# First attention: the causal mask moves from TensorE products to the VectorE instruction that takes the row maximum

## The reference

```
xn     = layernorm(x)
Wdkv   = xn @ latent_w + latent_b                 # keys and values, [b, 256, 36], shared by 16 heads
q      = xn @ Wd_w[h] + Wd_b[h]                   # [b, 16, 256, 36]
scores = q . Wdkv / sqrt(8), -inf where key > query
attn   = softmax(scores);  y = attn @ Wdkv;  out = concat(y) @ out_w + out_b
```

## Time and profile before

| | |
|---|---|
| median of the runs | 1755.04 us |
| span of the profiled execution, first to last instruction | 1746.9 us |
| what lies around the span (1755.04 less 1746.9) | 8.1 us |
| PE busy over the span | 1511.2 us (87%) |
| DVE busy over the span | 1119.7 us (64%) |
| ACT, POOL busy over the span | 997.0 us, 933.4 us |
| PE in the stretch 300 to 400 us (steady part of the first attention) | 98.71 us of 100 |
| DVE in the same stretch | 54.86 us of 100 |

### The profile page before, as it was taken

The page is one execution under the profiler, slowest core; times in us unless marked ns, Lnnn a source line. Parts: engine busy times, 40 slices in busy tenths (PEclk is TensorE's granted clock), DMA queues, the critical chain, the costliest instruction groups (busy, mean ns, idle before and its releaser), DMA issues. The chain is left out here.

```text
span 1746.9 us, 44836 instructions
## 1 busy us (share of the span) xinstructions
PE 1511.2 (87%) x14050; PEld 1109.0 (63%) x14051; DVE 1119.7 (64%) x2639; ACT 997.0 (57%) x2526; POOL 933.4 (53%) x1639
## 2 busy tenths in 40 slices
PE   4798999999999999998999488888888888885773
PEld 4655555555555555555998377777777777764662
DVE  3365555555555555553555399999899988985661
ACT  3343555555555555554332588888888888862441
POOL 6233555555555555554443666666666666632663
PEclk9998999999999999999999699999999999995875
DMA  7412222222222221223332021121211212116444
GB/s 197 133 29 57 55 55 55 55 55 55 56 56 56 56 56 56 56 59 75 68 70 60 22 49 45 41 44 43 46 43 41 44 44 45 42 31 123 89 90 113
DMA packets 240879, 107.53 MB, mean 62 GB/s; under 512 B 145465, under 2 KB 229242, under 8 KB 240762
## 3 DMA queue, kind: packets, MB, share of 16 engines
q1 hardware_dynamic: 230586, 93.23, 22.4%
q0 software_dynamic: 10240, 13.64, 3.7%
HBM read 61.92 MB, written 40.16 MB: 58 GB/s over the span
## 5 line engine op out<-in xcount | busy, mean ns | idle before, releaser
L670 POOL TENSOR_SCALAR_AFFINE_SELECT probs<-probs 128x512 f32<-128x512 f32 x256 | 183.5, 740 | 160.0 <-ACT probs L1515 160.0
L962 DVE TENSOR_REDUCE mneg<-bankS 128x2 f32<-128x256 f32 x256 | 107.2, 419 | 221.5 <-PE bankS L1848 220.9
L1515 ACT ACTIVATE probs<-bankT 128x1024 f32<-128x1024 f32 x128 | 131.0, 1023 | 185.2 <-PE bankT L1861 185.2
L963 DVE TENSOR_REDUCE mneg<-bankS 128x2 f32<-128x512 f32 x256 | 174.3, 681 | 0.0
L1510 ACT ACTIVATE qT<-bankA,bd 128x256 f32<-128x256 f32 x256 | 107.5, 473 | 95.0 <-PE bankA L1830 95.0
L1830 PE MATMUL bankA<-xnT,wd 128*128 128x256 f32 x512 | 149.7, 416 | 0.0
L663 POOL CAST qb<-qT 128x256 bf16<-128x256 f32 x256 | 97.1, 398 | 96.5 <-ACT qT L1510 96.3
L1858 PE MATMUL bankT<-qT,kT 37*128 37x512 f32 x512 | 136.9, 611 | 7.5 <-DMA qT<-mT 5.4
L1319 DVE STREAM_TRANSPOSE pt<-pe 128x768 f32<-128x768 f32 x128 | 124.4, 972 | 25.3 <-ACT pe L1600 25.1
L1875 PE MATMUL bankB<-probs,vaug 128*64 128x512 f32 x512 | 139.0, 621 | 1.1 <-ACT yT L1522 1.0
L1522 ACT COPY yT<-bankB 128x512 f32<-128x512 f32 x128 | 75.0, 586 | 82.1 <-PE bankB L1879 82.1
(11 more groups left out here) (316 smaller groups left out, 4315.6 us busy)
## 6 DMA issues: line engine op xcount, KB each, us to landing
rzb<-reciprocals SPq DMA_DIRECT2D x128, 128.0 KB
yT<-yT SPq DMA_DIRECT2D x64, 128.0 KB
xtab<-tab SPq DMA_DIRECT2D x32, 192.0 KB, 2.0
xs_sorted<-zeros SPq DMA_DIRECT2D x1, 4608.0 KB, 18.5
qT<-xs_sorted SPq DMA_DIRECT2D x144, 32.0 KB, 1.7
ys_sorted<-qT SPq DMA_DIRECT2D x36, 128.0 KB, 1.9
value_rows<-vrow SPq DMA_DIRECT2D x32, 128.0 KB, 1.8
vx<-value_rows SPq DMA_DIRECT2D x256, 16.0 KB, 1.8
```

Of the source, the lines that this page charges most:

```text
L670: pool.affine_select(out=blocks, in_=blocks, compare_op=ALU.is_ge, fill=0.0, base=0, pattern=[[0, 4], [1, P]], channel_multiplier=-1).then ...
L962: dve.tensor_reduce(mneg[:, n.half, :, j, 0], bankS[:, :, 0:128], AX.X, ALU.max, negate=True)
L963: dve.tensor_reduce(mneg[:, n.half, :, j, 1], bankS[:, :, 128:384], AX.X, ALU.max, negate=True).then_inc(S["red_done"], 1)
L1515: act.activation(pT[:, g % 2].rearrange("p e j t -> p e (j t)"), bankT[:, 0:2, :], ACT.Exp, scale=SCALE0).then_inc(S["exp_done"], 1)
```

## The change

The four mask products go, and with them `rowsel` and `rowneg`. A tile `future` (128 x 256, bf16; columns 0 to 127 zero, columns 128 to 255 zero or -1e30 above the diagonal) is added once, so that `future[:, 128:256]` masks the first query tile and `future[:, 0:256]` the second. `red` becomes one semaphore increment and four `tensor_tensor_reduce`, two per head, which add the mask to the scores, write the sum back to `bankS`, and write the maximum of each row, not negated, to `mpos`. The constant row from `lb` turns from 1 to -1, so that the second computation of the scores subtracts the maximum as before.

```diff
-        rowsel = sb("rowsel", [P, 2, P], BF16)
-        rowneg = sb("rowneg", [P, 2, LP], BF16)
+        future = sb("future", [P, T], BF16)
...
-            pool.affine_select(out=lb[:, :], in_=lb[:, :], compare_op=ALU.not_equal, fill=1.0, base=-L,
+            pool.affine_select(out=lb[:, :], in_=lb[:, :], compare_op=ALU.not_equal, fill=-1.0, base=-L,
...
-            for e in range(2):
-                r = HALVES[e]
-                pool.affine_select(out=rowsel[r, 0, :], in_=rowsel[r, 0, :], compare_op=ALU.not_equal, fill=1.0, base=0,
...
+            pool.affine_select(out=future[:, P:T], in_=future[:, P:T], compare_op=ALU.is_ge, fill=NEG, base=0,
+                               pattern=[[-1, P]], channel_multiplier=1)
...
             def red(n, j):
                 dve.wait_ge(S["s_ps"], n.b * PAIRS + (j + 1))
-                dve.tensor_reduce(mneg[:, n.half, :, j, 0], bankS[:, :, 0:128], AX.X, ALU.max, negate=True)
-                dve.tensor_reduce(mneg[:, n.half, :, j, 1], bankS[:, :, 128:384], AX.X, ALU.max,
-                                  negate=True).then_inc(S["red_done"], 1)
+                passed(dve)
+                for e in range(2):
+                    for t, keys in enumerate((slice(P, T), slice(0, T))):
+                        scores = bankS[:, e, t * P:t * P + (t + 1) * P]
+                        ins = dve.tensor_tensor_reduce(scores, scores, future[:, keys], 1.0, -3e38,
+                                                       ALU.add, ALU.max, mpos[:, n.half, e, j, t:t + 1])
+                ins.then_inc(S["red_done"], 1)
...
-                for k in range(2):
-                    for e in range(2):
-                        blocks = bankS[:, e, 0:384].rearrange("p (i h c) -> p i h c", h=2, c=LP)[:, 0:3:2, k]
-                        pe.matmul(blocks, rowsel[HALVES[e], k, :], rowneg[HALVES[e], k, :].unsqueeze(1).to_broadcast([LP, 2, LP]),
-                                  start=(k == 0), stop=False, skip_group_check=True)
                 for e in range(2):
-                    pe.matmul(bankS[:, e, 0:128], qb[ROWS[e], j, 0:P], kb[ROWS[e], 0:P], start=False, stop=True, skip_group_check=True)
+                    pe.matmul(bankS[:, e, 0:128], qb[ROWS[e], j, 0:P], kb[ROWS[e], 0:P], start=True, stop=True, skip_group_check=True)
                 for e in range(2):
-                    ins = pe.matmul(bankS[:, e, 128:384], qb[ROWS[e], j, P:T], kb[ROWS[e], :], start=False, stop=True, skip_group_check=True)
+                    ins = pe.matmul(bankS[:, e, 128:384], qb[ROWS[e], j, P:T], kb[ROWS[e], :], start=True, stop=True, skip_group_check=True)
```

More of the change, by code:

```diff
@@ L177, in program @@
         qb = sb("qb", [P, PAIRS, T], BF16)
-        mneg = sb("mneg", [P, 2, 2, PAIRS, 2])
+        mpos = sb("mpos", [P, 2, 2, PAIRS, 2])
         mT = sb("mT", [P, 2, 2 * H])
@@ L544, in _ @@
             pool.wait_ge(S["cst"], 1)
-            pool.affine_select(out=lb[:, :], in_=lb[:, :], compare_op=ALU.not_equal, fill=1.0, base=-L,
+            pool.affine_select(out=lb[:, :], in_=lb[:, :], compare_op=ALU.not_equal, fill=-1.0, base=-L,
                                pattern=[[0, 1]], channel_multiplier=1).then_inc(S["cst"], 1)
             pool.wait_ge(S["cst"], 2)
-            pool.affine_select(out=lb[:, :], in_=lb[:, :], compare_op=ALU.not_equal, fill=1.0, base=-(L + LP),
+            pool.affine_select(out=lb[:, :], in_=lb[:, :], compare_op=ALU.not_equal, fill=-1.0, base=-(L + LP),
                                pattern=[[0, 1]], channel_multiplier=1).then_inc(S["zeroed"], 1)
@@ L558, in _ @@
             pool.memset(identb[:, :], 0.0)
[L559 to L562, removed]
+            pool.memset(future[:, :], 0.0).then_inc(S["cst"], 1)
             pool.wait_ge(S["cst"], 3)
@@ L567, in _ @@
                                    pattern=[[-1, P]], channel_multiplier=1)
-            for e in range(2):
-                r = HALVES[e]
-                pool.affine_select(out=rowsel[r, 0, :], in_=rowsel[r, 0, :], compare_op=ALU.not_equal, fill=1.0, base=0,
[L571 to L583, removed]
+            pool.affine_select(out=future[:, P:T], in_=future[:, P:T], compare_op=ALU.is_ge, fill=NEG, base=0,
+                               pattern=[[-1, P]], channel_multiplier=1)
             pool.affine_select(out=strict[:, :], in_=strict[:, :], compare_op=ALU.is_gt, fill=0.0, base=0,
                                pattern=[[1, P]], channel_multiplier=-1).then_inc(S["consts"], 1)
-            made = 7
+            made = 3
             def chain(ins):
@@ L970, in turn_maxima @@
                 passed(dve)
-                dve.transpose(mT[:, n.half, :], mneg[:, n.half].rearrange("p e j t -> p (e j t)")).then_inc(S["mT_sb"], 1)
+                dve.transpose(mT[:, n.half, :], mpos[:, n.half].rearrange("p e j t -> p (e j t)")).then_inc(S["mT_sb"], 1)
             def invert(p):
```

## The result

Measured: 1802.75 us, median of four runs (1797.73 to 1803.42), against 1754.60 (1752.26 to 1758.58) before on the same chip: ratio 1.0263, interval 1.0231 to 1.0296. The kernel is 48 us slower; 1805 was forecast. The same kernel measured again gave 1.0258 (e8).

What follows compares the result with a forecast made beforehand. The single score buffer's loop between TensorE and VectorE was taken to hold three distances of a batch; the terms summed to +1.59 us a batch, +49 us in 31 steps, +1 us for the first batch: 1805 us, range 1754 to 1868.

Steps and rivals of the forecast that it cites:

- The loop: Round trip of the single score buffer bankS between TensorE and VectorE: 1.66 us a turn before, 2.09 forecast.
- The second result: Each new VectorE instruction also yields the row maximum, forecast as a step of its own costing 0.086 us, four times.
- r: Time from the first new VectorE instruction's start to the last one's end, forecast 1.46 us.
- The increment: Semaphore increment between VectorE's wait and the first new instruction, forecast to cost 0.12 us, between 0 and 0.15.
- TensorE's own distances: Pairs 2 to 3 and 4 to 5, set by TensorE's own work: 0.12 us less each, 2.77 forecast.
- Pair 6 to the keys' product: Batch's last distance, needing all eight maxima; normalise would delay the last one: 4.45 us in place of 4.10.
- The 8.1 us around the span: Difference between the profile's span of 1746.9 us and the median of 1755.04, taken as time around the span.
- half rate in PSUM: Fourth rival: VectorE reads and writes the same PSUM bank at half rate, 1955 us; chance 0.05.
- The other side: Second rival: what leaves TensorE outweighs what VectorE adds, 1750 or 1743 us; chance 0.06.
- w + r: Increment's cost plus the new instructions' time on VectorE; about 1.25 us decides between faster and slower.
- A second result without a step of its own: First rival: the maximum needs no extra instruction on VectorE, 1760 us; chance 0.25 for 1750 to 1780.
- dearer ones: Third rival: second results on VectorE cost more, 1831 us at 1.60 or 1901 at 1.96; chance 0.14.

Runs made afterwards that it cites:

- e1: The kernel before without its four mask products, its two maxima as before, taken over unmasked scores: 1738.01 us, ratio 0.9887.
- e3: The kernel before with only the one semaphore increment added between VectorE's wait and its first maximum: 1764.93 us, ratio 1.0049.
- e5: The changed kernel with one more tensor_tensor_reduce call over 128 columns ahead of the four, its result unused: 1844.81 us, ratio 1.0521.
- e2: The changed kernel with the mask products put back ahead of the score products, so the mask is added twice: 1821.22 us, ratio 1.0375.
- e4: The changed kernel with two products of constants into a free bank before pairs 1, 2, 4 and 6, results overwritten: 1790.27 us, ratio 1.0190.
- e6: The kernel before without mask products, and with the second normalise of a step moved behind the turned maxima: 1738.15 us, ratio 0.9912.

## Why the prediction was right

The sign, the size and the cause held: 48 us against 50. That the size came so close is luck: some terms were too dear, and the clock, which had no term, made up for them.

- **The loop is the bound: right, and shown.** Three edits that change the round trip by a known length (e1, e3, e5) move the turn by about that length (-0.11, +0.12, +0.2 us), and e2 shows the price of the new maximum with TensorE's work as before. The busy share of 98.74 had hidden it.
- **The second result: right that it is an instruction of its own, too dear in its cost.** The read takes 0.142 us in the mean (x1024), not 0.086, but three of the four lie beside the next main instruction: the reads add 0.14 us, not 0.34. The main instructions take 0.22, 0.38, 0.25 and 0.38 to what follows, 1.23 us where 1.12 was taken. These two errors go against each other, and r is 1.37 and not 1.46. The Trainium skill ("VectorE: DVE Perf Modes", section "Two Vector instructions with no wait between them") counts two instructions for such a call; the trace agrees (1024 main rows and 1024 reads), and adds that in this kernel only the last of four reads adds its whole length.
- **The increment: right.** 0.11 to 0.12 in e3's turn; 0.16 in the changed kernel (0.53 less 0.37), where 0.12 was taken. Together with r it makes the turn 2.05 instead of 2.09.
- **TensorE's own distances: right,** 2.78 and 2.77.
- **Pair 6 to the keys' product: wrong.** The step said that `normalise` would hold the last maximum, +0.35; it was +0.02 in the table and +0.06 in the mean (4.06 to 4.12). GpSimd's clip beside it, before and after (start, duration):

```profile
433.26 1.67 POOL L670 TENSOR_SCALAR_AFFINE_SELECT probs<-probs 128x512 f32<-128x512 f32 x2 [1.47 <-ACT probs L1515]
```

```profile
406.24 1.22 POOL L652 TENSOR_SCALAR_AFFINE_SELECT probs<-probs 128x512 f32<-128x512 f32 x2 [1.36 <-ACT probs L1501]
```

Before, `normalise` (433.37 to 434.43) lay wholly beside the clip and took 1.06 us; now it starts at 407.18, when the clip is nearly over (407.46), and takes 0.83. So it ends at 408.01, and the last maximum starts at 408.04, 0.53 us behind its scores (407.51): the loop's own delay. I had carried over a duration that belonged to a collision, to a place where the collision is nearly gone. It is worth about 9 us in all. What makes `normalise` long is not that it lies beside the clip but that it starts behind it. In e1 both start in the same moment, and it is the clip that grows:

```profile
404.93 0.68 DVE L982 TENSOR_TENSOR yT<-yT,rzb 128x512 f32<-128x512 f32 x1
```

```profile
404.93 1.76 POOL L670 TENSOR_SCALAR_AFFINE_SELECT probs<-probs 128x512 f32<-128x512 f32 x2 [1.36 <-ACT probs L1515]
```

Started 0.11 us behind the clip (before) `normalise` takes 1.06 us, 0.33 behind it (e3) 0.84, so that it ends 1.17 behind the clip's start in both. That reads as if the two engines took turns, and VectorE waited for the first of the clip's two selects to end; no run was made to test this.
- **The clock: missing.** The forecast had it at 1.00. The seven long batches are 11.6 us of the trace, and filling the waits gave 12 us back (e4). Without them the kernel stands at 1790 us, 15 below the forecast: 0.39 us a batch (1.59 less 1.20), 12 us in 31 steps, most of it the last point's, and the rest the first batches'.
- **The first batches: only a size.** +1.59 us in each of 31 steps was too simple; in the first ones a wait of 4.30 us for a DMA, and the half clock behind it, had room for most of it.
- **The 8.1 us around the span: wrong.** In the profiled executions here whose whole time is known, 1.4 to 2.9 us lie around the span (1.4 for the changed kernel). So the profile of before shows an execution some 6 us shorter than the median. The difference was not affected.

Rivals: half rate in PSUM is out: 256 columns go by in 0.38 us (404.12 to 404.50) with input and output in one bank. The other side, deciding at w + r of 1.25, did not come: it was 1.53. A second result without a step of its own (r = 1.20) and dearer ones (r from 1.60) are out with r = 1.37.

What stays open is why the clock falls only in every third or fourth batch, and why it fell in only one of 27 in e2, with TensorE as little busy and its waits as long. What differs there is the work between the waits, the mask products, and the length of a batch; no run separates these.

## What to carry to other kernels

When two engines take turns on one buffer, add up the turn from start to start, product, wait, maximum, release, and price a change by what it does to that sum; a busy share near 100% can hide the wait. Moving work from the "full" engine to the "free" one can be a loss if both stand in the same turn: here the turn gave back 0.12 us of products and took 0.16 us of increment and 0.34 us of longer maximum. A wait that is opened on TensorE may be paid a second time through its clock, and a duration read from a collision holds only as long as the collision does.

## What the hardware showed that was not expected

- The granted clock fell to half for a few us in one batch of three or four (394.4 to 397.7 us in the one shown), behind two waits of 0.65 and 0.37 us, while TensorE was busy 91% of the stretch; small products in the waits kept it up (e4).
- VectorE's product of two operands in SBUF and GpSimd's select hold each other up, and which of them pays goes by which starts first. `normalise` took 1.06 us started 0.11 us behind the clip, 0.84 started 0.33 behind it (e3), 0.83 beside the last 0.28 us of it, but 0.68 started together with it (e1) and 0.65 away from it (e6); the clip took 1.67 to 1.76 us with `normalise` started by its first 0.33 us, and 1.22 away from it or with `normalise` in its last 0.28 us.
- The accumulator's read takes 0.14 us behind a main instruction that writes PSUM and 0.08 behind one that writes SBUF (e5).
